# A Mamba-like scan and an expert layer on one core: the scan's state part added per channel ahead of the transposition, Toeplitz tables of two groups interleaved

## The reference

```python
xz = jnp.einsum('bld,ed->bel', hidden_states, W_in)          # 128 -> 2 x 256
x, z = jnp.split(xz, 2, axis=1)
x = silu(depthwise_conv(x, 4 taps) + conv_b)
k = _s4d_kernel(log_dt, log_A_real, A_imag, C_re, C_im, L)   # 256 kernels of 512 taps
y = jnp.fft.irfft(jnp.fft.rfft(x, n=n) * jnp.fft.rfft(k, n=n), n=n)[..., :L]
y = (y + x * D[None, :, None]) * silu(z)
x = _layernorm(x0 + jnp.einsum('bhl,dh->bld', y, W_out))
# then: 8 experts, relu(x @ w1[e] + b1[e]) @ w2[e] + b2[e] for the tokens whose argmax is e
x = _layernorm(x + moe(x))
```

## Time and profile before

| what | value |
|---|---|
| median of 3 runs | 269.93 us (267.04 to 270.8) |
| span of the profiled execution | 263.8 us, 6.1 us under the median of the runs; it has no time of its own but this span |
| PE busy, weight loads busy | 239.2 and 215.1 us |
| DVE, ACT, POOL busy | 177.0, 187.1, 139.8 us |
| moved by DMA | 52.06 MB |
| scan, from PE's first to its last matmul | 80.04 to 130.3 us |

### The profile page before, as it was taken

One profiled execution on the slowest core, in us unless ns is written; L12 is line 12 of the kernel. 1 busy time (PEld: TensorE's weight loads), 2 busy tenths in 40 slices (PEclk: granted clock), 3 DMA queues, 4 the chain that ended last, 5 costly groups with the idle time before them and its releaser, 6 DMA issues.

```text
span 263.8 us, 8892 instructions
## 1 busy us (share of the span) xinstructions
PE 239.2 (91%) x2763; PEld 215.1 (82%) x2764; DVE 177.0 (67%) x552; ACT 187.1 (71%) x528; POOL 139.8 (53%) x208
## 2 busy tenths in 40 slices
PE   8999979999999899999979999359989999999970
PEld 4888768888887678888869999349979999899960
DVE  1889995997218657777724878842877676566672
ACT  2999999856998778888655665207667777667740
POOL 6000000400009989999624687878746656657545
PEclk9999999999999999999999999759999999999995
DMA  7697884600399999999293221647865676677600
GB/s 232 180 313 288 346 334 150 244 0 0 105 310 332 310 279 296 308 320 302 66 361 120 93 93 41 212 92 191 220 179 172 200 210 164 203 195 208 189 34 6
DMA packets 54267, 52.06 MB, mean 197 GB/s; under 512 B 4415, under 2 KB 42817, under 8 KB 54114
## 3 DMA queue, kind: packets, MB, share of 16 engines
q1 hardware_dynamic: 51506, 46.65, 59.2%
q0 software_dynamic: 2304, 4.34, 4.6%
q10 hardware_dynamic: 432, 0.79, 0.8%
HBM read 38.14 MB, written 14.07 MB: 198 GB/s over the span
## 4 chain that ended last, share of the span: by engine, by line
PE 59%; DVE 10%; ACT 10%; POOL 9%; issue 6%; DMA 5%; SPq 1%; DVEq 0%; ACTq 0%; POOLq 0%
PE banks L1292 13%; PE banks L1477 9%; PE banks L1487 8%; PE banks L1370 7%; POOL dispatched_rows L568 5%; ACT BR L672 5%; PE banks L1380 5%; PE banks L1384 4%; PE banks L1275 3%; PE banks L1357 3%; PE banks L1435 2%; DMA X<-dispatched_rows 2%; POOL RE L558 1%; DMA out<-X 1%; POOL out L576 1%
## 5 line engine op out<-in xcount | busy, mean ns | idle before, releaser
L515 POOL TENSOR_TENSOR Wx<-BR,RE 128x384 f32 (+1 forms) x32 | 47.9, 1548 | 27.9 <-PE banks L1292 26.6
L1292 PE MATMUL banks<-Wx,XT 128*128 128x256 f32 x256 | 59.9, 380 | 1.7 <-ACT Z L643 1.7
L809 ACT ACTIVATE Z<-banks,BR 128x128 f32<-128x128 f32 x156 | 44.6, 368 | 18.4 <-PE banks L1477 18.3
L1292 PEld LDWEIGHTS banks<-Wx,XT 128*128 128x128 f32 x256 | 48.4, 190 | 9.0 <-issue 2.2
L576 POOL DMA_INDIRECT out<-X x39 | 38.4, 986 | 27.8 <-DVE X L1233 15.3
L1477 PE MATMUL banks<-Z 128*128 128x128 f32 x312 | 42.7, 281 | 0.4 <-ACT Z L798 0.2
L1487 PE MATMUL banks<-BR,Z 128*128 x312 | 41.1, 276 | 1.2 <-DVE X L1216 1.2
L1477 PEld LDWEIGHTS banks<-Z 128*128 128x128 f32 x312 | 39.0, 196 | 1.0 <-issue 0.5
L1487 PEld LDWEIGHTS banks<-BR,Z 128*128 128x128 f32 x312 | 37.8, 192 | 1.5 <-issue 1.5
L568 POOL DMA_INDIRECT dispatched_rows<-TR,CR x32 | 31.0, 970 | 9.3 <-POOL RE L558 9.3
L1057 DVE TENSOR_TENSOR X<-banks,Z 128x256 f32 (+1 forms) x32 | 20.4, 636 | 9.1 <-PE banks L1384 9.1
(11 more groups left out here) (220 smaller groups left out, 469.6 us busy)
## 6 DMA issues: line engine op xcount, KB each, us to landing
TR<-kernel_rows SPq DMA_DIRECT2D x32, 512.0 KB, 6.5
Z<-w SPq DMA_DIRECT2D x39, 256.0 KB, 3.1
dispatched_rows<-TR SPq DMA_DIRECT2D x3, 2310.0 KB, 8.8
X<-dispatched_rows SPq DMA_DIRECT2D x39, 66.0 KB, 2.1
XT<-hidden_t SPq DMA_DIRECT2D x10, 256.0 KB, 3.1
RE<-decay_and_turns SPq DMA_DIRECT2D x2, 1024.0 KB, 7.4
BR<-w SPq DMA_DIRECT2D x1, 2048.0 KB, 8.2
dispatched_rows<-TR SPq DMA_DIRECT2D x1, 1848.0 KB, 7.8
```

Of the source, the lines that this page charges most:

```text
L515: nc.gpsimd.tensor_tensor(BC[:, k, 0:LAGS, :].rearrange("p m (s r n) -> p (m s) r n", s=STRIPS, r=2), Btab[:, :, :, :, :, one].rearrange(" ...
L809: last = nc.scalar.activation(HT[:, j, c * P:c * P + P], bank[UP_BANKS[j]][:, c * P:c * P + P], ACT.Relu, bias=B1[:, bass.ds(experts[j] * ...
L1292: last = mm(bank[X_BANKS[k]][:, j * CHAN:(j + 1) * CHAN], XT[:, slot, at:at + CHUNK], Wx[:, tap, :], start=(tap == 0), stop=(tap == TAPS - 1))
```

## The change

It touches the scan alone, and the tables made for it.

- The state part is added to the conv product per channel, ahead of the transposition and in the same PSUM columns: 8 matmuls with 32 rows and 32 columns of weights (`V` of the channel's strip) and 128 moving columns (`Ctab`), `apply_states`. The one matmul of 192 moving columns and ACT's copy of its table fall away. PE's order is sum_states(g), convolve(g), turn_back(g-1), apply_states(g).
- `V` holds 2 channels of a strip in place of 8 with zeros between: DVE's `states` writes 48 elements in place of 192.
- The third lag of the state tables goes from POOL (2 lags, 128x256) to DVE (`last_lag`, 128x128).
- The kernel rows of two groups lie interleaved in DRAM, and one table of a pair of groups is loaded at once. The lower 64 rows of a table need only 64 columns; the other corner is zero and is set once by POOL. So a pair of groups takes two transfers, 512 KB to partitions 0 to 63 in pieces of 1024 bytes and 256 KB to partitions 64 to 127 in pieces of 512 bytes. There are 4 slots of a pair. The matmuls read every second element of the table.
- PE's 32 groups are written out; its loop is gone, and so is SP's.

```diff
@@ SP
-            def load_toeplitz(r, k):
-                group = r * T_SLOTS + k
-                    sp.wait_ge(s_tm, group - (T_SLOTS - 1))
-                sp.dma_start(Tring[:, k, :, :], toeplitz[:, bass.ds(group * GH, GH), :]).then_inc(s_t[k], 16)
+            def load_toeplitz(pair):
+                slot, home = pair % T_SLOTS, T_HOMES[pair % T_SLOTS]
+                wait_past(sp, s_tm, (pair - T_SLOTS) * 2 + 2)
+                sp.dma_start(Tring[0:HALF, home, :, :], toeplitz(pair, 0, CHUNK)).then_inc(s_t[slot], 16)
+                sp.dma_start(Tring[HALF:, home, :, 0:CHUNK], toeplitz(pair, HALF, HALF)).then_inc(s_t[slot], 16)
@@ POOL
-                    BC[:, k, 0:LAGS, :].rearrange("p m (s r n) -> p (m s) r n", s=STRIPS, r=2),
+                    BC[:, k, 0:POOL_LAGS, :].rearrange("p m (s r n) -> p (m s) r n", s=STRIPS, r=2),
...
+            def zero_corner(home):
+                nc.gpsimd.memset(Tring[HALF:, home, :, CHUNK:], 0.0).then_inc(s_tz, 1)
@@ ACT
             def group_product(r, k):
                 g = r * 2 + k
-                wait_past(act, s_y, g)
-                nc.scalar.activation(BC[:, k, LAGS, :], Ctab[:, bass.ds(g, 1), 1:KLEN].rearrange("p g j -> p (g j)"),
-                                     ACT.Copy).then_inc(s_cc, 1)
-                act.wait_ge(s_tm, g + 1)
+                act.wait_ge(s_ap, g + 1)
+                wait_past(act, s_y, g - 1)
@@ DVE
+                tt(BC[:, k, POOL_LAGS, :].rearrange("p (s r n) -> p s r n", s=STRIPS, r=2),
+                   Btab[:, POOL_LAGS, :, :, :, one].rearrange("p s r n g -> p s r (n g)"),
+                   falls.unsqueeze(2).to_broadcast([P, STRIPS, 2, PAIR * STATES]), ALU.mult).then_inc(s_bl, 1)
+            def group_turn(r, k, tables):
+                states(r, k)
+                if tables:
+                    last_lag(r + 1, k)
+                if k:
+                    output(r, 0)
+                else:
+                    output(r - 1, 1)
@@ PE
+            def apply_states(g):
+                k = g % 2
+                pe.wait_ge(s_v, g + 1)
+                for h in range(GH):
+                    at = slice(h // PAIR * STRIP, (h // PAIR + 1) * STRIP)
+                    last = mm(product_of(k, h), V[at, k, h % PAIR, :], Ctab[at, g, 0:CHUNK], start=False, stop=True)
+                last.then_inc(s_ap, 1)
...
-            with pe.Fori(0, GROUPS // T_SLOTS) as r:
-                for k in range(T_SLOTS):
-                    convolve(r, k)
-                    sum_states(r, k)
-                    finish(r, k - 1)
+            convolve(0)
+            sum_states(0)
+            apply_states(0)
+            for g in range(1, GROUPS):
+                sum_states(g)
+                convolve(g)
+                turn_back(g - 1)
+                apply_states(g)
```

More of the change, by code:

```diff
@@ L88, in build, with toeplitz @@
           gate_b, expert_bias, w1, b1, w2, b2, out):
-    kext = nc.dram_tensor("kernel_rows", [CHAN, KROW], F32).ap()
+    kext = nc.dram_tensor("kernel_rows", [P, KROW, 2], F32).ap()
     rows_dram = nc.dram_tensor("decay_and_turns", [2, P * GROUPS], F32).ap()
-    toeplitz = bass.AP(kext.tensor, 0, [[1, P], [KROW, CHAN], [1, CHUNK]])
+    def toeplitz(pair, first, columns):
+        return bass.AP(kext.tensor, pair * GH * KROW * 2 + first * 2, [[2, HALF], [KROW * 2, GH], [1, 2 * columns]])
     slots_dram = nc.dram_tensor("dispatched_rows", [SLOT_ROWS, ROW], F32).ap()
@@ L1055, in output @@
                 dve.wait_ge(s_zs, r + 1)
-                dve.wait_ge(s_y, g + 2)
-                tt(group, bank[4 + k][:, 0:GH * TILES].rearrange("p (h t) -> p h t", h=GH), gates, ALU.mult).then_inc(s_yc, 1)
+                dve.wait_ge(s_y, g + 1)
+                tt(group, bank[TURNED_BANKS[k]][:, 0:GH * TILES].rearrange("p (h t) -> p h t", h=GH), gates, ALU.mult).then_inc(s_yc, 1)
+            dve.wait_ge(s_bs, LAGS * 2)
+            dve.wait_ge(s_be, LAGS)
+            for k in range(2):
+                last_lag(0, k)
             dve.wait_ge(s_a, PAIRS)
@@ L1365, in convolve @@
+            def convolve(g):
+                k, pair = g % 2, g // 2
+                slot = pair % T_SLOTS
                 pe.wait_ge(s_xg, g + 1)
-                pe.wait_ge(s_t[k], (r + 1) * 16)
-                pe.wait_ge(s_yt, g + (LEAD - 1))
+                if k == 0:
+                    pe.wait_ge(s_tz, min(pair, T_SLOTS - 1) + 1)
+                    pe.wait_ge(s_t[slot], (pair // T_SLOTS + 1) * 32)
+                wait_past(pe, s_yt, g - 1)
                 for h in range(GH):
-                    at, part = h // 4 * P, h % 4 * TILES
-                    last = mm(yt[part:part + TILES, at:at + P], xg[:, h, :], Tring[:, k, h, :], start=True, stop=True)
+                    last = mm(product_of(k, h), XG[:, k, h, :], Tpairs[:, T_HOMES[slot], h, :, k], start=True, stop=False)
@@ L1387, in _, with turn_back @@
+            def turn_back(g):
+                k = g % 2
+                pe.wait_ge(s_yt, g + 1)
+                wait_past(pe, s_yc, g - 1)
+                for j in range(2):
+                    last = nc.tensor.transpose(bank[TURNED_BANKS[k]][:, j * P:(j + 1) * P], YT[:, k, j * P:(j + 1) * P], ident[:, :])
+                last.then_inc(s_y, 1)
             pe.wait_ge(s_xb, PAIRS - 1)
@@ L1390, in _ @@
             pe.wait_ge(s_const, 3)
-            pe.wait_ge(s_yt0, 1)
-            with pe.Fori(0, GROUPS // T_SLOTS) as r:
-                for k in range(T_SLOTS):
-                    convolve(r, k)
-                    sum_states(r, k)
-                    finish(r, k - 1)
+            convolve(0)
[6 more added lines that the diff above has]
+                apply_states(g)
             pe.wait_ge(s_ctr, 2)
             pe.wait_ge(s_late, 64)
-            mm(bank[2][:, 0:EXPERTS], centre[:, 0:DM], gwT[:, :], start=True, stop=True).then_inc(s_gwp, 1)
-            finish(GROUPS // T_SLOTS - 1, T_SLOTS - 1)
+            mm(bank[6][:, 0:EXPERTS], centre[:, 0:DM], gwT[:, :], start=True, stop=True).then_inc(s_gwp, 1)
+            turn_back(GROUPS - 1)
             pe.wait_ge(s_gw, 1)
```

174 lines of the change are left out of this document (92 added, 82 removed).

## The result

The changed kernel takes 297.79 us (median of 5 runs, 296.15 to 303.13), the kernel before 269.69 us (5 runs, 267.04 to 270.80) on the same chip: ratio 1.108, interval 1.100 to 1.116. The forecast was 284.2 us. The sign and the cause were right; the loss is 28.1 us where 14.3 were forecast. A ratio leaves out, on either side, the few runs that were clearly longer than the others of the same kernel.

A forecast was written before the change was run, and what follows sets the result against it. The prediction took late supply of TensorE's written-out program as deciding: 14 pieces at 4.2 us end the scan at 144.6 against 130.3, 14.3 us more on 263.8, plus 6.1 from span to median: 284.2 us, range 268 to 301.

The forecast's parts named there:

- The supply of program: TensorE's scan: written-out program arrives in pieces of 241 matmuls and weight loads, each serving 2.08 groups; 14.3 us more.
- TensorE's own pace: TensorE's scan: its own instructions take 1.45 to 1.60 us a group.
- the estimated 0.1 for a change of shape: TensorE's scan: one more step from the full matmul shape to a small one costs about 0.1 us a group.
- the doubled element step: Convolve's reads of every second table element: taken as nothing, bounded by another 0.46 us a group.
- last_lag and the lock: VectorE's scan steps: last_lag often waits for GpSimd's table, up to 1.03 us, giving 1.55 us a group.
- T: Time from one piece of TensorE's program to the next in the scan: 4.2 us; chance 0.50 for 3.6 to 4.9.
- The upper bound of the same paragraph, 5.45: Longest time between program pieces in the scan, 5.45 us, from one stop's end to the next in the earlier trace.
- The clock stays granted: TensorE in the scan: a sign of the forecast being right, its clock remaining granted.
- (a): Scan: program supply keeps up, T at most 3.2; 270.5 us, no change; chance 0.22 with neighbours up to T = 3.55.
- (b): Scan: supply keeps up, apply_states overlaps by pairs, last_lag seldom meets GpSimd; 1.35 us a group, 264 us; chance 0.07.
- (c): Scan: program supply stays as slow as in the first turn, T = 5.45; 302 us; chance 0.18 together with (d).
- (d): Scan: half-partition table transfers bind, 5.5 us a pair at half the present rate; 301 us; chance 0.18 together with (c).

The follow-up runs named there:

- e1: Changed kernel with TensorE's scan as a loop of four turns, waiting for VectorE's states ahead of the transpositions; 1.04 to 1.07 of the kernel before.
- g1: Changed kernel with TensorE's scan as a loop, the wait for VectorE's states kept behind the transpositions; 1.042 of the kernel before.
- e4: Kernel before with only TensorE's scan loop written out, 32 groups of 88 matmuls and weight loads; 1.034 of the kernel before.
- e2: Changed kernel without the table loads of pairs 4 to 15, so its output is not the reference's; 1.047 of the kernel before.
- g3: Changed kernel with TensorE's scan looped, the states' wait behind the transpositions, and all three lags' tables on GpSimd; 1.033 of the kernel before.
- h3: Changed kernel, still written out, with VectorE's last_lag behind the output; 1.116 of the kernel before.
- e3: Changed kernel with each pair's table loaded by one transfer over all 128 partitions, without zeroing the corner; 1.097 of the kernel before.
- g4: Changed kernel with TensorE's scan looped, the states' wait behind the transpositions, and tables loaded over all 128 partitions; 1.039 of the kernel before.
- h1: Changed kernel with every second table load of pairs 4 to 15 left out, so its output is not the reference's; 1.092 of the kernel before.
- f2: Changed kernel with TensorE's scan looped, the states' wait ahead of the transpositions, and VectorE's last_lag behind the output; 1.056 of the kernel before.
- g2: Changed kernel with TensorE's scan looped, the states' wait behind the transpositions, and VectorE's last_lag behind the output; 1.035 of the kernel before.
- f4: Kernel before with only the third lag's table moved from GpSimd to VectorE, after the output; 1.001 of the kernel before.

## Why the prediction came out as it did

**The bound and its cause: right.** The supply of program was named as the term that decides; e1 and g1 (no stops behind the first turn, a scan 20 and 22 us shorter), e4 (a loss of the same kind, 10.2 us, with nothing else changed) and e2 show it. The piece of 241 instructions was 246, and of the 14 to 15 packets forecast 15 start from 87.38 to 161.91. Seven of the eight stops were 1.0 to 3.1 us, where 0.5 to 1.5 were forecast.

**TensorE's own pace, 1.45 to 1.60, taken 1.55: right,** at its upper end; 1.59 in g3. Convolve took 0.58, not 0.46, and the transpositions 0.37, not 0.27; the estimated 0.1 for a change of shape was part of that. How much is the doubled element step, which the forecast put at nothing, no run shows.

**last_lag and the lock, 1.55 a group: right in mechanism, a little short.** It took 1016 ns on average beside a table of 1096 ns, and in g1 held the pace at 1.67. In the changed kernel it cost nothing (h3).

**The step that failed: "Scaling the 2.8 us by 0.55 to 0.6: 2.55 + 1.65 = 4.2 us. I take T = 4.2."** The wait between TensorE's going on and the next packet was taken as proportional to queue 1's load, and so put at 1.65 us in place of 2.8. The load itself came out near the forecast (67.1% of the DMA engines' time from 86 to 153, 0.55 to 0.6 forecast). But the wait did not shrink: behind the seven stops of over 1 us it was 3.85, 3.36, 3.70, 2.02, 2.52, 1.52 and 2.36 us, 2.8 on average, as before; with the 2.55 to 2.9 us from a packet's start to TensorE's going on that makes 5.4. With no loads at all (e2) it was still 2.2, 2.4 and 2.0 us behind the three long stops, and the pieces came every 3.99 us, where the scaling would have left 2.55.

From the end of the first piece (passed at 85.2) to 160.56 there are fourteen pieces in 75.4 us, T = 5.38. 14 x (5.38 - 4.2) gives 16.5 us more. The first piece ends 2.8 us later than the 82.4 forecast, because the scan begins 1.6 us later and the first states take 2.0 us and not half a microsecond; what comes behind the last piece is 0.8 us shorter. That is the whole error on the trace: TensorE ends at 163.15 in place of 144.6. In the medians the error is 13.6 us, 5 us less, for a reason that is not the forecast's merit: it added the 6.1 us by which the profiled run of the kernel before lay under its median, while the changed kernel's span of 298.0 lies 0.2 over its own.

T lies outside the 3.6 to 4.9 that had the chance of 0.50. The upper bound of the same paragraph, 5.45, was the better value; the earlier trace rows had only loaded examples, and nothing in the trace showed a piece without load.

**"The clock stays granted": wrong.** It fell to the lower level behind most of the long stops. By h3 it is more a symptom than a cost: some 4 us of the scan's 31.

**The rivals.** (a) and (b) did not happen; the page's sentence that the fetch is mostly hidden (the Trainium skill, Runtime: NRT & Kernel Launch, "Instruction fetch mechanics") does not hold for these stretches, in which TensorE still stood for up to 0.5 us at a piece with idle DMA engines (e2, from 104 on). (c), 302 us with T = 5.45, was nearest in its mechanism. (d), 301 us, was not the cause: TensorE never waited for a table, and e3 and g4 changed nothing of weight. The Trainium skill's "The DMA port swizzle" (SBUF - State Buffer) is borne out in the rate: the half-partition loads moved 229 GB/s from 80 to 90 (203 in e1), and the full ones of the kernel before 334 there, with the DMA engines full in all three; but the rate was not on the path.

**What stays open.** What in the table traffic delays a piece: behind stops of over 1 us the wait for the next packet was 2.8 us with all of it, and 2.2 with none, and h1's 5.3 us mixes the traffic with the clock. The request for a piece and the load of the next pair both follow TensorE's progress, about once in two groups each, and may meet for that reason; this was not tried.

No version beat the kernel before. The nearest that keeps the change, g3, loses 3%, 8.7 us at that chip's 268.2: in the profiles 8.1 us, of them 0.12 us a group by TensorE's 116 instructions (2.9 us in the later 24), 2.8 us in the first eight groups (16.8 us against 14.0), whose program must be fetched, and 2.4 us by a later start (82.4 against 80.0).

## What to carry to other kernels

Count the instructions of TensorE's written-out stretches: here 246 matmuls and weight loads were one 16 KB piece, which came every 4.0 us without table loads and every 5.4 to 5.7 us beside them. TensorE, which would go through 72 of these small instructions a microsecond (116 in 1.6 us), got some 45; the same work in a loop of 928 had no long stop behind its first turn (0.3 us at most). When an engine looks full beside another, relieve it in one cheap run before building on it: GpSimd's 28.0 of 28.0 us was a coincidence. And when an edit moves a wait, look first at who now waits there: e1's early wait hid the very effect that f2 was to measure.

## What the runs showed of the hardware

- A product of 128 elements on VectorE with both inputs in SBUF took 1016 ns where GpSimd's table of 1096 ns had begun before it, and 437 ns where it began ahead of the table (g2). In the changed kernel it begins 0.3 us behind the table and ends 0.25 us behind it:

```profile
110.63 1.02 DVE L1072 TENSOR_TENSOR Wx<-BR,RE 128x128 f32 x1
```

```profile
110.34 1.06 POOL L521 TENSOR_TENSOR Wx<-BR,RE 128x256 f32 x1 [3.88 <-PE banks L1398]
```

and in g2 it begins 0.2 us ahead and is done in 0.43 us:

```profile
113.28 0.43 DVE L1090 TENSOR_TENSOR Wx<-BR,RE 128x128 f32 x1
...
113.47 1.20 POOL L525 TENSOR_TENSOR Wx<-BR,RE 128x256 f32 x1 [0.49 <-PE banks L1416]
```

- At a stop TensorE goes on 1.2 to 1.7 us after the end of a packet, with table loads (the changed kernel, e4) and without (e2); a packet itself mostly takes 0.9 to 1.4 us. What varies is the time ahead of it.
- The stops fall at fixed places of the program, every 246 to 247 matmuls and weight loads, the same ones in the changed kernel and in e2.
- Chips of the same kind differed by 3 to 5% on the same kernel (268.0, 268.2 and 269.7 against 278.5 and 281.1 us), mostly behind the scan; the pace in the scan was the same (1.46 us a group in f4, on the slowest).
